# Moving the loads of the scores' moving operand to GpSimd's queue, and rearranging both ends of an attention kernel

## Reference

```
y = layernorm(x)                       # (b, t, 128), heads of 8 channels
scores = einsum('bhtk,bhsk->bhts', y_h, y_h) / sqrt(8)
attn = softmax(scores)                 # over s
o = einsum('bhts,bsc->bhtc', attn, y)  # each head attends over all 128 channels
x = x + layernorm(o.reshape(b, t, 16 * 128) @ weight)
z = layernorm(x); zp = z shifted by one token
r = sigmoid((mu_r * z + (1 - mu_r) * zp) @ W_r.T)
k = relu((mu_k * z + (1 - mu_k) * zp) @ W_k.T) ** 2
x = x + layernorm(r * (k @ W_v.T))
```

## Time and profile before

| | |
|---|---|
| median of 3 runs | 937.39 us (937.16 to 938.22) |
| profiled execution | 938.51 us, its span 936.7 us |
| PE busy | 909.5 us (97%) |
| DVE busy | 864.2 us (92%) |
| ACT busy | 755.9 us (81%) |
| POOL busy | 213.2 us (23%) |
| DMA queues' share of 16 engines | GpSimd's (software) 73.9%, the hardware ones' 15.4% |
| granted clock of PE | 0.997 |

### The profile page before, as it was taken

The page is one execution under the profiler, slowest core; times in us unless marked ns, Lnnn a source line. Parts: engine busy times, 40 slices in busy tenths (PEclk is TensorE's granted clock), DMA queues, the critical chain, the costliest instruction groups (busy, mean ns, idle before and its releaser), DMA issues.

```text
span 936.7 us, 17734 instructions
## 1 busy us (share of the span) xinstructions
PE 909.5 (97%) x6057; PEld 440.1 (47%) x6057; DVE 864.2 (92%) x1207; ACT 755.9 (81%) x1052; POOL 213.2 (23%) x344
## 2 busy tenths in 40 slices
PE   4999999999999999999999999999999999999995
PEld 2344444445444445444444454444554444544453
DVE  7999898999899999999889999999989998999977
ACT  7878788788788878888778878888878887788855
POOL 2111241221131412312122323222113131131210
PEclk9999999999999999999999999999999999999998
DMA  7999989999899988999899898899989998999830
GB/s 216 200 223 185 210 176 217 217 196 204 180 185 201 186 178 175 210 191 222 177 183 189 181 200 170 176 223 212 192 179 180 201 184 167 186 183 200 168 68 24
DMA packets 100618, 173.65 MB, mean 185 GB/s; under 512 B 21040, under 2 KB 63408, under 8 KB 100528
## 3 DMA queue, kind: packets, MB, share of 16 engines
q0 software_dynamic: 36576, 133.19, 73.9%
q1 hardware_dynamic: 63952, 39.32, 15.4%
HBM read 28.77 MB, written 10.49 MB: 42 GB/s over the span
## 4 chain that ended last, share of the span: by engine, by line
PE 90%; SPq 4%; DVE 2%; DMA 1%; ACT 1%; issue 1%; POOLq 0%; DVEq 0%; POOL 0%; ACTq 0%
PE ps_o L577 25%; PE ps_o L579 22%; PE ps_o L578 22%; PE ps_s L558 8%; PE ps_r L593 3%; PE ps_r L595 3%; PE ps_r L594 3%; SPq L321 2%; SPq L328 2%; PE ps_x L610 1%; PE ps_x L620 1%; PE ps_x L616 1%; DMA op_t<-scr_t 1%; ACT e_f L744 0%; DMA scr_s<-yT 0%
## 5 line engine op out<-in xcount | busy, mean ns | idle before, releaser
L1121 DVE TENSOR_TENSOR e_lo<-e_f,e_hi 128x2048 f16<-128x2048 f32 x256 | 583.7, 2280 | 33.1 <-DMA e_hi<-e_f 32.3
L744 ACT ACTIVATE e_f<-ps_s 128x2048 f32<-128x2048 f32 x256 | 481.3, 1880 | 145.6 <-PE ps_s L558 136.9
L577 PE MATMUL ps_o<-e_hi,y_hi 128*128 128x512 f16 x1024 | 391.2, 382 | 0.1
L578 PE MATMUL ps_o<-e_lo,y_hi 128*128 128x512 f16 x1024 | 388.6, 379 | 0.0
L579 PE MATMUL ps_o<-e_hi,y_lo 128*128 128x512 f16 x1024 | 388.5, 379 | 0.0
L415 POOL DMA_DIRECT2D e_hi<-e_f x254 | 137.7, 542 | 672.9 <-ACT e_f L744 601.6
L577 PEld LDWEIGHTS ps_o<-e_hi,y_hi 128*128 128x128 f16 x1024 | 99.7, 97 | 149.0 <-issue 48.0
L579 PEld LDWEIGHTS ps_o<-e_hi,y_lo 128*128 128x128 f16 x1024 | 100.3, 98 | 121.3 <-issue 0.6
L756 ACT ACTIVATE part<-ps_r,rden 128x128 f32<-128x128 f32 x500 | 142.4, 374 | 14.3 <-DVE rden L1133 14.0
L578 PEld LDWEIGHTS ps_o<-e_lo,y_hi 128*128 128x128 f16 x1024 | 100.4, 98 | 91.4 <-issue 0.9
L558 PE MATMUL ps_s<-op_t,op_s 32*128 32x512 f16 x1024 | 102.5, 388 | 4.8 <-ACT e_f L744 2.8
(11 more groups left out here) (236 smaller groups left out, 421.1 us busy)
## 6 DMA issues: line engine op xcount, KB each, us to landing
e_hi<-e_f POOLq DMA_DIRECT2D x254, 512.0 KB, 4.9
op_t<-scr_t SPq DMA_DIRECT2D x496, 32.0 KB, 3.7
op_s<-scr_s SPq DMA_DIRECT2D x496, 16.0 KB, 3.4
scr_s<-yT SPq DMA_DIRECT2D x12, 256.0 KB, 4.3
scr_t<-yT SPq DMA_DIRECT2D x12, 256.0 KB, 5.1
out_dram<-res SPq DMA_DIRECT2D x7, 256.0 KB, 4.7
xs<-in_L_attn_x_dram SPq DMA_DIRECT2D x3, 512.0 KB, 6.8
w_last<-in_L_attn_weight_dram SPq DMA_DIRECT2D x1, 1024.0 KB, 11.6
```

The lines of the kernel that those rows point to most:

```text
L577: nc.tensor.matmul(dst, y_hi[:, b % 2, s, :], e_hi[:, ring, g, :], start=(q == 0 and g == 0), stop=False)
L578: nc.tensor.matmul(dst, y_hi[:, b % 2, s, :], e_lo[:, ring, g, :], start=False, stop=False)
L744: nc.scalar.activation(e_f[:, k % EF_RING], ps_s[:], ACT.Exp, scale=1.0 / ROOT).then_inc(weighed, 1)
L1121: dve.tensor_tensor(flat(e_lo[:, ring]), flat(e_f[:, k % EF_RING]), flat(e_hi[:, ring]), ALU.subtract).then_inc(split, 1)
```

## The change

It has three parts.

**Loads.** The four `op_t` DMAs of a step are issued by POOL's queue, right behind the cast of an odd quad k (of step (k - 1)/2 + 4; of steps 4 and 5 behind casts 3 and 4); SP keeps the four of `op_s`. PE waits on a semaphore for each.

**Start.** Batch 0 writes first only the part of the scratch that steps 4 to 15 read; the remaining writes follow at k 15, 17 and 19, and the scratch eighths of batch 1 move from k 8 to 12 to k 21 to 27, the load of x of batch 1 from k 6 to 11. `weight_base` is spread as 4, 3, 3, 3, 3 over k 3 to 7 (before 8, 4, 4). products(0) to products(3) are split in halves: of products(1) to (3) the first half stands ahead of score(5) to (7), the second half behind. `take_second_t` is split over k 3 and 4.

**Tail.** Row 6's last newton goes from DVE to POOL. The key of the last row is formed by two matmuls from `zT`, shifted and not, with weights scaled beforehand on POOL, so that ACT's scaled copies (L932, L933) and DVE's key mix go. PE's order is key(0), key(1), gate(0), kv(0), gate(1), kv(1) (before key(0), gate(0), key(1), gate(1), kv(0), kv(1)). Centring of the gated product goes from DVE (L1340) to ACT, DVE making only the negated mean. One memset ahead of the last splits takes the place of two, and both last reciprocals come ahead of the add of the step before.

```diff
+            def kept(b):
+
+                return (slice(FIRST * HS, P), slice(0, BANK)) if b == 0 else (slice(0, P), slice(0, T))
...
                 for i in (0, 1):
-                    sp.dma_start(scr_s[b][:, i, :], yT[:, 0, :]).then_inc(scr_s_in[b], 16)
+                    sp.dma_start(scr_s[b][rows, i, :], yT[rows, 0, :]).then_inc(scr_s_in[b], 16)
                 for i in (0, 2):
-                    sp.dma_start(scr_t[b][:, i, :], yT[:, 0, :]).then_inc(scr_t_in[b], 16)
+                    sp.dma_start(scr_t[b][rows, i, cols], yT[rows, 0, cols]).then_inc(scr_t_in[b], 16)
...
+            def keep_late_s():
+                rows = slice(0, FIRST * HS)
+                for i in range(3):
+                    sp.dma_start(scr_s[0][rows, i, :], yT[rows, i // 2, :]).then_inc(scr_late, 16)
+
+            def keep_late_t(i):
+                cols = slice(BANK, T)
+                src = shT[:, cols] if i == 3 else yT[:, i % 2, cols]
+                sp.dma_start(scr_t[0][:, i, cols], src).then_inc(scr_late, 16)
...
                 for g in range(4):
-                    sp.dma_start(*op_s_load(j, g)).then_inc(op_in[slot], 16)
-
-            def load_t(j):
-                slot = j % OP_RING
-                if j == FIRST or j % (2 * H) == 0:
-                    sp.wait_ge(scr_t_in[batch_of(j)], 4 * 16)
-                for g in range(4):
-                    sp.dma_start(*op_t_load(j, g)).then_inc(op_in[slot], 16)
+                    sp.dma_start(*op_s_load(j, g)).then_inc(op_s_in[slot], 16)
...
-                if k in (8, 10, 12):
-                    keep_eighth((k - 6) // 2)
-                if k in (6, 20, 34):
-                    b = (6, 20, 34).index(k) + 1
+                if k == 15:
+                    keep_late_s()
+                if k in (17, 19):
+                    for i in range(k - 17, k - 15):
+                        keep_late_t(i)
+                if k in (21, 23, 27):
+                    keep_eighth((21, 23, 27).index(k) + 1)
+                if k in (11, 20, 34):
+                    b = (11, 20, 34).index(k) + 1
...
+            def load_t(j):
+                slot = j % OP_RING
+                ge(pool, scored, 2 * (j - OP_RING + 1))
+                if j == FIRST or j % (2 * H) == 0:
+                    pool.wait_ge(scr_t_in[batch_of(j)], 4 * 16)
+                if j == H:
+                    pool.wait_ge(scr_late, 7 * 16)
+                for g in range(4):
+                    nc.gpsimd.dma_start(*op_t_load(j, g)).then_inc(op_t_in[slot], 16)
+
+            def step_loaded(k):
+
+                if k in (3, 4):
+                    return FIRST + k - 3
+                j = (k - 1) // 2 + OP_RING
+                return j if k % 2 and FIRST + 2 <= j < STEPS else None
...
                 if ROUNDED <= k < QUADS:
                     cast(k)
+                j = step_loaded(k)
+                if j is not None:
+                    load_t(j)
...
+            def last_newton():
+                v, y, a, bias = (fnw[:, 2, n, :] for n in range(4))
+                pool.wait_ge(f_near[2], 2 * LAST_ROW)
+                step(nc.gpsimd.tensor_tensor(a, y, y, ALU.mult))
...
+                for n, share in ((0, mu), (1, mu_rest)):
+                    nc.gpsimd.tensor_scalar(l_key_w[:, n, :], wT[:, 1, :], share[:, 1:2], None,
+                                            ALU.mult).then_inc(l_key_w_ok, 1)
+
+            last_newton()
+            last_key_weights()
...
-                    pe.wait_ge(op_in[slot], op_loaded(j))
+                    pe.wait_ge(op_s_in[slot], op_loaded(j))
+                    pe.wait_ge(op_t_in[slot], op_loaded(j))
...
-                if k == LAG + 1:
-                    products(1, range(2))
+                if LAG + 1 <= k <= LAG + 3:
+                    products(k - LAG, range(2))
                 if k < QUADS:
...
                 if k == LAG - 1:
-                    products(0)
-                if k == LAG + 1:
-                    products(1, range(2, 4))
-                if 2 <= k - LAG < QUADS:
+                    products(0, range(2))
+                if LAG <= k <= LAG + 3:
+                    products(k - LAG, range(2, 4))
+                if 4 <= k - LAG < QUADS:
                     products(k - LAG)
...
-                pe.wait_ge(l_mix_k, u + 1)
-                nc.tensor.matmul(half_ps("key", u), wT[:, 1, :], mix[:, 1, wide(u)], start=True,
-                                 stop=True).then_inc(l_key_ps, 1)
+                now = zT[:, 1 + WIDE * u:1 + WIDE * (u + 1)]
+                prev = zT[:, WIDE * u:WIDE * (u + 1)]
+                pe.wait_ge(l_zT, u + 1)
+                pe.wait_ge(l_key_w_ok, 2)
+                pe.wait_ge(prev_ok, ROWS)
+                nc.tensor.matmul(half_ps("key", u), l_key_w[:, 0, :], now, start=True, stop=False)
+                nc.tensor.matmul(half_ps("key", u), l_key_w[:, 1, :], prev, start=False, stop=True).then_inc(l_key_ps, 1)
...
-            last_key(0)
-            last_gate(0)
-            last_key(1)
-            last_gate(1)
-            last_kv(0)
-            last_kv(1)
+            for u in range(HALVES):
+                last_key(u)
+            for u in range(HALVES):
+                last_gate(u)
+                last_kv(u)
...
                     take_first_s(1)
-                    take_second_t()
+                    take_second_t(SET)
+                if k == 4:
+                    take_second_t(SET + 1)
...
-                act.wait_ge(rest_ok, 1)
-                nc.scalar.activation(l_rest[:, 1, wide(u)], prev, ACT.Copy, scale=mu_rest[:, 1:2]).then_inc(l_rest_k, 1)
-                nc.scalar.activation(l_rest[:, 0, wide(u)], prev, ACT.Copy, scale=mu_rest[:, 0:1]).then_inc(l_rest_r, 1)
+
+            def last_centre(u):
+                act.wait_ge(l_minus, u + 1)
+                act.wait_ge(l_gated, u + 1)
+                for k in range(PAIR * u, PAIR * (u + 1)):
+                    ins = nc.scalar.activation(l_mid[:, 1, k, :], gated[:, k, :], ACT.Identity, bias=l_neg[:, k:k + 1])
+                ins.then_inc(l_mid_ok[1], 1)
 
...
+            for u in range(HALVES):
                 last_sigmoid(u)
             nc.scalar.activation(idle[:], consts[:, 0:1], ACT.Sqrt)
+            last_centre(0)
             last_sqrt(2, slice(0, RB), HALVES)
+            last_centre(1)
...
-                if o in (6, 16, 35):
+                if o in (6, 16) or o == 35 and r < LAST_ROW - 1:
                     row_newton((6, 16, 35).index(o), r)
...
                     weight_columns()
-                    for h in range(H // 2):
+                    for h in range(H // 4):
                         weight_base(h)
-                if k in (4, 5):
-                    for h in range(H // 4):
-                        weight_base(H // 4 * (k - 2) + h)
+                if 4 <= k < 8:
+                    for h in range(3):
+                        weight_base(3 * k - 8 + h)
...
+                    sums_at = (17, 18, 19, 20) if b == 1 else (12, 13, 17, 18)
+                    if o in sums_at:
+                        first = 2 * sums_at.index(o)
                         batch_sums(b, range(first, first + 2))
...
+            def last_clear():
+                dve.wait_ge(added, LAST_STEP - 1)
+                dve.memset(last_acc[:, :, C - 1:C], 0.0).then_inc(l_full, 1)
...
-                dve.memset(a[:, pair(u), C - 1:C], 0.0).then_inc(l_full, 1)
-                dve.wait_ge(l_full, u + 1)
-                last_sums(0, pair(u), a)
+                dve.wait_ge(l_full, 1)
+                last_sums(0, pair(u), last_acc)
...
-                for i, rest, ready in ((1, l_rest_k, l_mix_k), (0, l_rest_r, l_mix_r)):
-                    dve.wait_ge(rest, u + 1)
-                    dve.scalar_tensor_tensor(out=mix[:, i, wide(u)], in0=now, scalar=mu[:, i:i + 1],
-                                             in1=l_rest[:, i, wide(u)], op0=ALU.mult, op1=ALU.add).then_inc(ready, 1)
+                dve.wait_ge(mix_k, LAST_ROW)
+                dve.tensor_tensor(mix[:, 2, wide(u)], now, prev, ALU.subtract).then_inc(l_mix_d, 1)
+                dve.wait_ge(l_mix_d, u + 1)
+                dve.scalar_tensor_tensor(out=mix[:, 0, wide(u)], in0=mix[:, 2, wide(u)], scalar=mu[:, 0:1], in1=prev,
+                                         op0=ALU.mult, op1=ALU.add).then_inc(l_mix_r, 1)
 
...
+            last_clear()
             for u in range(HALVES):
                 last_split(u)
             last_invert(0)
-            add(LAST_STEP - 1)
             last_invert(1)
+            add_near()
             for u in range(HALVES):
...
             for u in range(HALVES):
                 last_gated(u)
-                last_centre(1, 2, pair(u), gated, u + 1)
+                last_minus(u)
```

More of the change, by code:

```diff
@@ L165, in sandwich @@
         scr_const = sem("scr_const")
+        scr_late, mu_in = sem("scr_late"), sem("mu_in")
         scr_s_in = [sem(f"scr_s_in_{b}") for b in range(B)]
```

(49 more changed lines are left out.)

57 lines of the change are left out of this document (31 added, 26 removed).

## The result

The changed kernel took 941.47 us (median of 7 runs, 939.54 to 942.02) against 937.61 us before; the ratio is 1.0035, 95% interval 1.0022 to 1.0047. It is slower, where 934.5 was forecast.

The account below looks back on a forecast made before the run. The prediction took PE to bound the kernel, 90% of the chain. From the profiled 938.51, start -1.3, steady part +0.2 and tail -1.8 gave 935.6, or 934.5 as median; range 932.8 to 940.0.

Parts of the forecast that it names:

- What bounds the kernel, and the cover: Steady part: PE is busy 400 of 400 us, and a cast may come 3.0 to 3.4 us late before PE feels it.
- Loads on POOL: Steady part: four loads behind each odd cast leave the even cast on time; with tight quads 0 to 5 us, taken 0.2.
- The price per load: POOL's issue of one `op_t` load, taken as 0.53 us, the price of a steady cast.
- The stretch of `y_lo`: POOL's `y_lo` of 4.65 us is mostly waiting, so a start 2.1 us later hardly moves its end.
- D: Rival, chance 0.10: at 1.46 us per load issue POOL needs 6.90 us per step, above 6.72; 22 us lost, 956.
- B: Rival, chance 0.24: only the tail gains, the start held by ACT gives 0 to 0.5; 935.8, up to 937.
- C: Rival, chance 0.12: casts wait behind loads in POOL's queue, `e_hi` lands later every second quad; at 2.4 us delay 946.
- The rule weighed there: DMAs issued by GpSimd can starve while VectorE holds the shared port; by it a loss of tens of us.
- Start: First 75 us: waits removed less what split products cost, net -1.3 us, from -3.4 to +0.6.
- The `op_t` waits: Start: scores' 1.6 us of waits for `op_t` loads go once POOL issues them, -1.6 us.
- So the halves trade a wait for another: +0.3: Start, split products: score(4) 0.85 us earlier, score(8) at 36.5 to 37.1; +0.3 us, from -1.8 to +0.6.
- Tail: End of the kernel: earlier last split -1.07, memsets -0.1, key -0.4, centring -0.2; sum -1.77 us, from -1.2 to -2.2.

Follow-up runs that it names:

- dodge: The changed kernel, but where POOL has tensor operations in an iteration, that step's loads wait for the next, behind the even cast: 0.9987 of before.
- tiny_loads: The kernel before, its own loads on SP, plus four unread 32 x 64-byte loads issued by POOL behind each odd cast: 1.0034 of before; repeated, 1.0058.
- tail_only: The kernel before with the tail's edits alone, loads on SP and start as before: 0.9969 of before; repeated, 0.9971.
- tail_halves: The kernel before, loads on SP, with the tail's edits, split products, spread `weight_base` and split `take_second_t`: 0.9983 of before.
- tail_dodge_late: The kernel before with the tail's edits, `op_t` loads on POOL as in `dodge`, and batch 1's x load, sums and scratch eighths later: 0.9969 of before.

## Why the prediction was wrong, point by point

**What bounds the kernel, and the cover.** Right: PE had next to no waits in the steady part before, a steady cast had 3 us of cover, and the loss came as PE waits behind `e_lo` and `o_neg`, which the prediction names as the sign that it is wrong.

**Loads on POOL: the step that failed.** The price per load was right (0.53 forecast, 0.512 measured), as was POOL's total ("near 50%", 51%). The step that failed is "Four of them behind the odd cast make 0.53 + 4 x 0.53 = 2.65 us. ... the even cast comes about 3.0 us behind the odd one, so it is not late: cost 0". It left 0.35 us free in each gap and then counted only `y_lo` among POOL's other work there. In 12 odd iterations POOL has tensor operations in the same gap as the loads, three with `y_lo` and nine with the two operations of a newton step, 1.5 us and more. Late casts went from 8 to 32. In place of the forecast 0.2 us the steady part cost 7.2 in the trace, of which 0.7 to 3.7 also show with the loads on SP, and 5.6 to 6.3 us by `dodge` beside the changed kernel. (The stretch of `y_lo`, taken as cover, did not absorb the loads: at 134.33 it took 1.17 us for 4.65 before, but the `e_lo` beside it took 3.93 for 2.29 and PE waited 0.79 at 140.09; in batches 2 and 3 the `y_lo` behind the loads took 2.82 and 2.84 us for 1.19 and 1.60.) `tiny_loads` shows the time as cause, `dodge` the placement. POOL's stops of 2.5 us at "issue", which the forecast didn't know, are in `dodge` still (six); its steady part lost 2.4 us from score(20) on, no more than kernels with the loads on SP, so their cost isn't distinguishable from nothing.

**Rivals.** D had the resource right, POOL's time, and put its price in the single issue; it wasn't needed. B had the start right, which gained nothing (below). C, transfers ahead of casts in POOL's queue, is refuted: in quads 176 to 250, where few other things move, casts landed in 4.9 and 5.0 us (odd, even) on average, both before and after.

The rule weighed there, from the Trainium skill, "SBUF — State Buffer", section "SBUF: two separate sides", speaks of VectorE's fast modes; the prediction applied it to any busy VectorE. POOL's issues of loads took 0.51 us beside a VectorE 92% busy, so nothing starved here. Which of VectorE's operations run in a fast mode no trace here shows, so the rule itself is neither borne out nor refuted. What did stretch are POOL's tensor operations, such as the 3.76 us above.

**Start.** The trace has -1.2 at score(20) against a forecast of -1.3, but that is chance. `tail_only`, `tail_only_again` and `tiny_loads_again` have the start's products and scratch writes of before and are 1.1 to 1.8 us ahead of the same profile of before. The `op_t` waits went, as forecast; one wait of 1.68 us for an exp took the place of several:

```profile
36.81 0.40 PE L618 MATMUL ps_s<-op_t,op_s 32*128 32x512 f16 x4 [1.68 <-ACT e_f L809]
```

score(8) came at 36.81, inside the 36.5 to 37.1, and as the profiles above show that is some 0.7 us later than with the start of before: the term that was too small is "So the halves trade a wait for another: +0.3". It walked score(4) rightly, which comes 0.1 to 0.9 us sooner, but took the exps behind it too lightly. By the ratios the split products and what came with them cost 0.0012 to 0.0018 (`tail_halves` to `tail_only`, `dodge` to `tail_dodge_late`). Missed too was what the dates are worth: with loads on POOL they keep some 3 to 6 us that would be lost. They were not priced; before's trace shows no collision, which I put down to SP being late there (its x load starts at 43.04).

**Tail.** Right in mechanism, the term too small: 2.6 against 1.8. It is the firmest number here: from the last reciprocal of four columns to the end of the span it takes 24.7 us in before and 22.0 to 22.1 in all 13 profiles with the new tail. VectorE's timeline:

```profile
917.97 0.18 DVE L1205 RECIPROCAL rden<-ps_r 128x4 f32<-128x4 f32 x1 [0.79 <-PE ps_r L655]
918.08 0.41 DVE L1389 SCALAR_TENSOR_TENSOR o_neg<-o_hi,ps_o 128x256 f16<-128x256 f16 x1
...
932.78 0.42 DVE L1471 SCALAR_TENSOR_TENSOR gated<-gate,ps_x 128x256 f32<-128x256 f32 x1 [0.85 <-PE ps_x L765]
...
934.04 0.17 DVE L1429 TENSOR_SCALAR l_neg<-l_mv 128x2 f32<-128x2 f32 x1
...
936.61 1.14 DVE L1444 SCALAR_TENSOR_TENSOR xn<-w_raw,l_w,yn 128x128 f32<-128x128 f32 x4
```

Reciprocal to split went from 1.31 to 0.11 (-1.20, forecast -1.07). From `z` to gated(0) it is 4.80 in place of 5.57 (-0.77, forecast -0.4): it didn't end at the 0.69 of idle time, since VectorE's own mix ahead became shorter, and it idles 0.85 now. gated(0) to the last group is 3.83 for 4.26 (-0.43, forecast -0.2). The remaining -0.2 lie in the layernorm between.

## What to carry to other kernels

When work moves to an engine with time to spare, count the gap it goes into with everything that engine does there, iteration by iteration; an average of 23% busy hid the 12 gaps that had no room. If those can be named, put the moved work elsewhere: the same loads one iteration later, and with the other dates as in the change, cost nothing that could be measured.

A queue that is late also delays what stands behind it. Before freeing it, look at the next large transfer in its order and ask what it will meet when it starts sooner.

A term that comes out as forecast in one pair of profiles isn't confirmed by that. Lay the profiles of kernels beside it that lack the edit: here they show the same gain.

## What the hardware showed that I had not expected

Four DMAs of 32x512 and one of 128x512 with the same bytes aren't alike: the one costs POOL 0.72 instead of 2.0 us, but the median landing of the casts rises from 5.1 to 5.7 us, and the ratio from 1.0035 or 1.0054 to 1.0125. Four issues of 64-byte rows cost POOL as much (0.511 us each) as four of 1 KB rows (0.512). POOL stops for 2.5 us about every 130 us once it issues 750 DMAs, with two stops in all in the profile of before, at 254. Tensor operations of POOL beside a busy VectorE take very different times: the same copy of one column of `zT` 2.29 us before and 5.13 after (5.12 in `tail_only`, with the loads on SP), a newton operation of 128x8 1.67 to 3.76; and VectorE's `e_lo` once took 3.93 instead of 2.29 us beside POOL's `y_lo`.
